# A two-layer graph kernel: layer 1's attention loop taken by pairs of units, in bfloat16 halves

## The chip, the cores and the metric

The kernel runs on one core of one Trainium2 chip. The metric is the time of one execution on the device, in microseconds; the kernel before takes 824.5 us (median of 3 runs, 824.09 to 824.69).

## The reference

x is 2708 x 128 and adj a 0/1 matrix of 2708 x 2708. Both layers end in a layer norm.

```python
# layer 0: x = layernorm(x + diffusion + sigmoid(alpha) * (softmax(beta * sim * adj) @ x - x))
# layer 1, with A = adj and X the result of layer 0:
XW = X @ W
s_col = XW @ a[0, :f]; s_row = XW @ a[0, f:]
Z1  = leaky_relu(s_row[:, None] + s_col[None, :], negative_slope=0.01)
den = exp(Z1)
num = A @ den
att = where(num != 0, den / where(num != 0, num, 1.0), 0.0)
H   = A @ (att @ XW)
x   = layernorm(X + H)
```

## The kernel before

Nodes are padded to 22 tiles of 128; the free axis of 2708 columns is cut into six chunks of 452 or 448 columns (`CH`). AT holds the transposed adjacency in SBUF as bfloat16. The order of the work is written out by hand: each engine has its own program, and engines meet only at semaphores, so an engine that waits holds up everything behind it in its program. The PE (TensorE) writes PSUM, which has eight banks.

**Layer 0** (until about 241 us) computes the softmax attention. Its last part ("the tail of layer 0", 241 to 372 us) runs over 22 row tiles: PE multiplies AT by x (`spread`, L1298), DVE (VectorE) adds the parts and takes mean and variance (`norm_in`: L797, L799, and L801 which adds epsilon), POOL (GpSimd) takes the power -0.5 (L391), and one tile later DVE subtracts the mean and multiplies (`x1_rows`, L809). Between these DVE runs the ranking steps (L832 to L854) by which both keys of layer 1 are sorted.

**Between the layers** (372 to 460 us) rows of AT are gathered in the sorted order by POOL's indirect DMAs (L411), and PE computes block sums (L1411). Since both keys are sorted, exp of the leaky relu splits into sums over blocks above and below a threshold, taken from a table `tab` (one product, L1471), except in the few tiles that the threshold crosses. For these the dense values `den` are computed, and multiplied with AT in a loop over tiles whose bounds are read into registers (L1478).

**Layer 1's loop** (460.6 to 728.8 us) has 132 units (`UNITS`): 22 column tiles `jt` times six chunks. PE goes by pairs `v` of units, 66 in all: `num(v)` puts two numerators into banks 6 and 7: two table products (L1471), four products for each crossed tile (two bfloat16 parts of `den` for each of two chunks, L1478), and two tiny closing matmuls (L1482). For each unit ACT (ScalarE) takes the logarithm (L589), DVE forms the score z (L1122) and subtracts the logarithm (L1136), ACT takes the exponential with a bias (L595), and PE multiplies by XW in float32 (L1492) into banks 0 to 5, two pairs behind `num` (`LAG`). There are seven slots for z and three for logarithms, of 452 columns each. DVE forms two scores ahead:

```python
for u in (2 * v, 2 * v + 1):
    if u + 2 < NU:
        attention_scores(u + 2)
    dv.wait_ge(s_ln, u + 1)
    V.tensor_tensor(z_of(u), z_of(u), l_of(u), ALU.subtract)
```

Once for each `jt`, `den_scores` (L1052, L1056) prepares the next tile's `den` on DVE behind two register loads and a branch, ACT takes its exponential (L568), and `den_halves` splits it (L1067, L1069). `den_all` (not entered here) is a branch in the third pair of each `jt`.

XW in sorted order comes by 22 indirect DMAs that POOL issues from 461.5 us on (L417), after the last block sum; the product of tile `jt` waits for its own DMA only.

**The end**: banks 0 to 5 are copied to YT (DVE L1147, ACT L603), transposed by PE (L1505), copied again (L1156, L608), written to DRAM in two DMAs (SP, L302 and L305), gathered by 22 indirect DMAs of POOL (L427), split by DVE (L759, L761) in four slices (`SL`), and multiplied with AT (L1516 for the first six row tiles, slice by slice; `spread`, L1298, for the other 16). The layer norm follows, with the power on POOL (L433) and the last step on DVE (L1173).

## Time and profile before

| | us |
|---|---|
| median of 3 runs | 824.5 |
| profiled execution | 824.38 |
| its span on the core | 822.6 |
| PE busy | 702.5 (85%) |
| DVE busy | 649.6 (79%) |
| ACT busy | 448.6 (55%) |
| POOL busy | 284.4 (35%) |

The profiled execution takes 1.8 us more than its span; it lies within the three runs. Busy shares are averages over stages that have different limits, so the stages are to be looked at one by one. Matmuls are pipelined: the duration of one is longer than the distance to the next, and the distance is what a stream of them costs. Of the 22 column tiles of layer 1's loop, 19 have two crossed tiles, one (jt 8) has three, and two (jt 20 and 21) have one, as the count of L1478 between two table products shows (8, 12 and 4).

### The profile page before, as it was taken

The page shows a single profiled execution, that of the slowest core. Times are in us where ns is not written, and L with a number is a line of the kernel's source. Part 1 is how long each engine was busy: PE and PEld are TensorE (multiplying, and loading weights), DVE is VectorE, ACT ScalarE, POOL GpSimd, SP SyncE. Part 2 cuts the span into 40 slices and gives each one's busy share as a digit, 9 for nine tenths or more (in the row PEclk, how much of TensorE's full clock was granted, in tenths as well). Part 3 has the DMA queues.
Part 4 walks back from the last instruction along what each step waited for, and adds up shares of the span by engine and source line. Part 5 has one row for each costly group of instructions (what it writes and reads, how often), then busy time and mean ns, then how long its engine had stood idle before and what let it go on. Part 6 is the DMA issues. An engine that isn't in the chain of part 4 may idle for free.

```text
span 822.6 us, 13449 instructions
## 1 busy us (share of the span) xinstructions
PE 702.5 (85%) x4380; PEld 385.1 (47%) x4380; DVE 649.6 (79%) x1428; ACT 448.6 (55%) x705; POOL 284.4 (35%) x294
## 2 busy tenths in 40 slices
PE   5599999999969888843799899999999999965895
PEld 5243334333338777732345344444444444433684
DVE  3599999999987799998966778776777777862584
ACT  2398888888851156785202466665666666740000
POOL 5378888787760211112820460000000000007431
PEclk9999999999977999955799999999999999986998
DMA  9953454980000000021970010000000000023110
GB/s 209 207 98 68 78 92 77 408 328 1 1 4 1 14 22 14 14 84 52 372 321 0 24 49 0 1 1 0 1 2 1 0 2 1 0 71 120 32 39 20
DMA packets 24552, 58.22 MB, mean 71 GB/s; under 512 B 2634, under 2 KB 13918, under 8 KB 24478
## 3 DMA queue, kind: packets, MB, share of 16 engines
q0 software_dynamic: 7744, 33.39, 16.0%
q1 hardware_dynamic: 16734, 23.92, 8.1%
q8 instruction: 37, 0.61, 0.3%
q14 instruction: 37, 0.30, 0.1%
HBM read 51.59 MB, written 20.96 MB: 88 GB/s over the span
## 4 chain that ended last, share of the span: by engine, by line
PE 54%; DVE 28%; issue 10%; POOL 3%; ACT 2%; DMA 2%; DVEq 0%; POOLq 0%; SPq 0%; ACTq 0%
PE PSALL L1492 14%; PE PSALL L1478 13%; PE PSALL L1298 8%; DVE ring L724 7%; DVE R L733 6%; PE PSALL L1411 5%; PE PSALL L1471 3%; PE PSALL L1278 2%; DVE R L845 2%; PE PSALL L1226 2%; POOL X L427 2%; DVE XN L845 1%; PE PSALL L1354 1%; PE PSALL L1516 1%; PE PSALL L1482 1%
## 5 line engine op out<-in xcount | busy, mean ns | idle before, releaser
L369 POOL TENSOR_TENSOR R<-R,ring 128x452 f32<-128x452 f32 (+1 forms) x126 | 151.6, 1204 | 33.2 <-ACT ring L462 31.5
L733 DVE SCALAR_TENSOR_TENSOR R<-ring,R 128x452 bf16<-128x452 f32 (+1 forms) x132 | 134.6, 1021 | 0.0
L1478 PE MATMUL PSALL<-AT,R 128*128 x516 | 117.4, 355 | 4.1 <-issue 1.4
L1278 PE MATMUL PSALL<-R,AO 128*128 128x452 bf16 (+2 forms) x396 | 98.9, 359 | 16.8 <-DVE R L733 15.7
L462 ACT ACTIVATE ring<-ring,sm 128x452 f32<-128x452 f32 (+1 forms) x132 | 88.4, 670 | 27.8 <-DVE ring L724 21.0
L1226 PE MATMUL PSALL<-XN 128*128 128x452 f16 (+2 forms) x396 | 98.4, 358 | 4.7 <-issue 4.2
L1298 PE MATMUL PSALL<-R,AT 128*128 128x256 f16 (+1 forms) x836 | 102.1, 284 | 0.0
L470 ACT ACTIVATE R<-ring,sm 128x452 bf16<-128x452 f32 (+1 forms) x132 | 88.6, 671 | 4.3
L1298 PEld LDWEIGHTS PSALL<-R,AT 128*128 128x128 bf16 (+1 forms) x836 | 83.8, 102 | 12.8 <-issue 0.2
L1492 PE MATMUL PSALL<-ring,X 128*128 128x452 f32 (+1 forms) x188 | 84.8, 567 | 0.0
L423 POOL MEMSET R<- 128x108 f32 x1 | 0.2, 188 | 237.9 <-PE PSALL L1492 237.9
L724 DVE TENSOR_TENSOR ring<-PSALL,AT 128x452 f32<-128x452 f32 (+1 forms) x132 | 81.0, 614 | 0.9 <-PE PSALL L1226 0.9
L1478 PEld LDWEIGHTS PSALL<-AT,R 128*128 x516 | 49.4, 96 | 65.0 <-issue 40.8
L595 ACT ACTIVATE ring<-ring,st 128x452 f32<-128x452 f32 x94 | 62.9, 671 | 25.4 <-DVE ring L1136 25.4
L1122 DVE SCALAR_TENSOR_TENSOR ring<-R,st 128x452 f32<-128x452 f32 x94 | 64.1, 682 | 0.0
L1278 PEld LDWEIGHTS PSALL<-R,AO 128*128 128x128 bf16 (+1 forms) x396 | 28.5, 97 | 73.9 <-DVE R L733 59.6
L1226 PEld LDWEIGHTS PSALL<-XN 128*128 128x128 f16 (+1 forms) x396 | 32.6, 97 | 51.0 <-DVE ring L724 28.4
L1411 PE MATMUL PSALL<-AT,X 128*128 128x452 bf16 (+1 forms) x264 | 53.0, 362 | 2.2 <-DVE X L984 2.2
L391 POOL TENSOR_TENSOR ln<-ln,sm 128x1 f32<-128x1 f32 (+1 forms) x22 | 13.7, 621 | 97.4 <-DVE ln L801 97.4
L529 ACT ACTIVATE XN<-R 128x128 bf16<-128x128 bf16 (+20 forms) x28 | 37.9, 1354 | 15.7 <-DVE R L845 14.1
L589 ACT ACTIVATE ring<-PSALL,sm 128x452 f32<-128x452 f32 x44 | 27.8, 633 | 26.9 <-PE PSALL L1482 26.9
L1492 PEld LDWEIGHTS PSALL<-ring,X 128*128 128x128 f32 x188 | 32.0, 189 | 19.5 <-issue 18.0
(247 smaller groups left out, 1100.1 us busy)
## 6 DMA issues: line engine op xcount, KB each, us to landing
AT<-in_adjT POOLq DMA_DIRECT2D x22, 677.0 KB, 7.4
ATd<-AT SPq DMA_DIRECT2D x2, 7447.0 KB, 31.0
XWd<-ring SPq DMA_DIRECT2D x11, 128.0 KB, 1.8
x1d<-AO SPq DMA_DIRECT2D x1, 1408.0 KB, 5.8
out<-ring SPq DMA_DIRECT2D x21, 64.0 KB, 1.5
Yd<-R SPq DMA_DIRECT2D x1, 768.0 KB, 3.7
Yd<-R SPq DMA_DIRECT2D x1, 640.0 KB, 3.6
AT<-ATd,idx POOLq DMA_INDIRECT x22, 10.4
```

Of the source, the lines that this page charges most:

```text
L369: i = G.tensor_tensor(ES_, ES_, z, ALU.add)
L462: S.activation(z, z, ACT.Exp, scale=bcol[0:rows, :]).then_inc(s_exp, 1)
L470: S.activation(fh, z, ACT.Identity, bias=mone[0:rows, :]).then_inc(s_exp, 1)
L724: V.tensor_tensor(z, PSALL[0:rows, b, 0:w], A_, ALU.mult).then_inc(s_z, 1)
L733: V.scalar_tensor_tensor(F[0:rows, RW:RW + w], z, 1.0, F[0:rows, 0:w], ALU.subtract, ALU.subtract).then_inc(s_low, 1)
L1122: V.scalar_tensor_tensor(z_of(u), rb[:, c0:c0 + w], c99[:, jt:jt + 1], rb01[:, c0:c0 + w], ALU.add, ALU.max).then_inc(s_z1, 1)
L1226: m = TE.matmul(PSALL[0:rows, b, 0:w], lh[:, jt * P:jt * P + rows], rh[:, c0:c0 + w], start=(k == 0), stop=(k == 2))
L1278: m = TE.matmul(PSALL[:, c, 0:w], half_[0:rows, jt, :], F[0:rows, o:o + w], start=(jt == 0 and k == 0), stop=(jt == T - 1 and k == 2))
L1298: ins = TE.matmul(PSALL[0:m, bank, 0:2 * D], AT[:, jt, it * P:it * P + m], parts[:, jt, :, :].rearrange("p c d -> p (c d)"), start=(jt == ...
L1411: m = TE.matmul(PSALL[:, c, 0:w], W3[q][:, t * P:(t + 1) * P], AT[:, t, c0:c0 + w], start=(t == 0 and q == 0), stop=(t == T - 1 and q == 1))
L1478: TE.matmul(PSALL[:, b, 0:w], d, AT[:, bass.ds(k, 1), c0:c0 + w].rearrange("p o j -> p (o j)"), start=False, stop=False)
L1492: TE.matmul(PSALL[:, c, 0:CH[c][1]], XWs[:, jt, :], z_of(u), start=(jt == 0), stop=(jt == T - 1)).then_inc(s_y, 1)
```

## The change

Layer 1's loop goes by pairs on all engines. A score, a logarithm, a subtraction and an exponential now cover two chunks, 904 (or 900) columns, in one instruction. There are four slots for z and one for the logarithm. The term of slope 0.01 of the row is taken out of the loop (`erb`, multiplied in when PSUM is read at the end) and that of the column too, so the score is a tensor_scalar (add, max with 0) and the exponential has no bias.

The exponential's float32 is read as two bfloat16 halves in place: the upper 16 bits are `high`, and DVE writes z minus high into the lower 16 bits (`attention_low`, new; one per pair). POOL splits XW in the same way (`XWh`, three instructions a tile), after it has issued all 22 indirect DMAs. The product of a unit becomes three bfloat16 matmuls in place of one in float32.

Where exactly two tiles are crossed, `num` runs eight products and the two table products in line, without loop and closing matmuls; otherwise the old loop runs. `den` is split in place too: three tensor_scalar, one exponential, one subtraction.

At the end DVE alone reads the six banks, pair by pair as they are done, PE transposes into six banks of their own, ACT alone copies them; eight row tiles, not six, are multiplied slice by slice. The last step of both layer norms moves from DVE to POOL, with the addition of epsilon, and DVE's tensor_reduce of the last tail becomes a scalar_tensor_tensor. Small operations between the layers are rearranged.

```diff
+        den_w = R1[:, DEN0:DEN0 + NDEN * P].rearrange("p (t j) -> p t j", t=NDEN)
+        den_h = R1[:, DEN0:DEN0 + NDEN * P].bitcast(BF16).rearrange("p (t j c) -> p t j c", t=NDEN, c=2)
...
-        slots = [ring[:, 5, :], R1[:, rest:rest + RW]] + [AO[:, q * RW:(q + 1) * RW] for q in range(3)]
-        slots += [ring[:, q, :] for q in range(5)]
-        NZ, NL = 7, 3
-        tL, tZ = slots[0:NL], slots[NL:]
+        pairs = [RF[:, 0:2 * RW], RF[:, 2 * RW:4 * RW], AO[:, 0:2 * RW], RF[:, 4 * RW:6 * RW]]
+        NZ = 4
+        tL = R1[:, rest:rest + 2 * RW]
+        XWh = X[:, :].bitcast(BF16).rearrange("p (t d c) -> p t d c", t=T, c=2)
...
+        def halves_of(v):
+
+            both = z_of(v).bitcast(BF16).rearrange("p (n c) -> p n c", c=2)
+            return both[:, :, 1], both[:, :, 0]
...
+                mean, var, rstd = moments(it)
+                gp.wait_ge(s_tail, TAIL * it + 4)
+                G.tensor_scalar(rstd, var, LN_EPS, None, ALU.add).then_inc(s_rstd, 1)
+                gp.wait_ge(s_rstd, 2 * it + 1)
+                G.tensor_tensor(rstd, rstd, mhalf[0:m, :], ALU.pow).then_inc(s_rstd, 1)
+                gp.wait_ge(s_ao, 12)
+                if it == T - 1:
+                    G.memset(AO3[:, it, :], 0.0).then_inc(s_x1, 1)
+                    gp.wait_ge(s_x1, T)
+                gp.wait_ge(s_rstd, 2 * it + 2)
+                G.tensor_scalar(AO3[0:m, it, :], hc[0:m, s, :], mean, rstd, ALU.subtract, ALU.mult).then_inc(s_x1, 1)
...
+            gp.wait_ge(s_ohl[1], T)
+            gp.wait_ge(s_perm[1], 2)
+            for t in range(T):
+                gp.wait_ge(s_AT[t], 48)
+                if t:
+                    gp.wait_ge(s_xws, 3 * t)
+                G.tensor_copy(iota[:, :], XWs[:, t, :]).then_inc(s_xws, 1)
+                gp.wait_ge(s_xws, 3 * t + 1)
+                G.tensor_tensor(XWh[:, t, :, 0], XWs[:, t, :], iota[:, :], ALU.subtract).then_inc(s_xws, 1)
+                gp.wait_ge(s_xws, 3 * t + 2)
+                G.tensor_copy(XWh[:, t, :, 1], iota[:, :]).then_inc(s_xws, 1)
...
+            gp.wait_ge(s_y, NV)
+            gp.wait_ge(s_sub, NV)
+            G.memset(YT[:, N:NP], 0.0).then_inc(s_pad, 1)
...
-                for u in (2 * v, 2 * v + 1):
-                    av.wait_ge(s_num, u + 1)
-                    if u < NL:
-                        av.wait_ge(s_E, 1)
-                        av.wait_ge(s_winset, 2)
-                    else:
-                        av.wait_ge(s_sub, u - NL + 1)
-                    av.wait_ge(s_const, CONST)
-                    S.activation(l_of(u), PSALL[:, 6 + u % 2, 0:CH[UNITS[u][1]][1]], ACT.Ln, bias=tiny).then_inc(s_ln, 1)
+                av.wait_ge(s_num, v + 1)
+                if v:
+                    av.wait_ge(s_sub, v)
+                else:
+                    av.wait_ge(s_E, 1)
+                av.wait_ge(s_const, CONST)
+                S.activation(tL.rearrange("p (q w) -> p q w", q=2), PSALL[:, 6:8, 0:RW], ACT.Ln, bias=tiny).then_inc(s_ln, 1)
                 if cp == 0 and jt + 1 < T:
                     den_exp(jt + 1, 0)
-                for u in (2 * v, 2 * v + 1):
-                    av.wait_ge(s_sub, u + 1)
-                    av.wait_ge(s_c99, 2)
-                    S.activation(z_of(u), z_of(u), ACT.Exp, bias=c01[:, jt:jt + 1]).then_inc(s_att1, 1)
+                av.wait_ge(s_sub, v + 1)
+                S.activation(z_of(v), z_of(v), ACT.Exp).then_inc(s_att1, 1)
...
+                    for q in range(WN):
+                        V.tensor_scalar(den_w[:, s + q, :], cb3[:, jt, :], rsrt[:, q:T][:, bass.ds(where["base"], 1)],
+                                        r01[:, q:T][:, bass.ds(where["base"], 1)], ALU.add, ALU.max).then_inc(s_denz, 1)
...
-                    V.tensor_copy(den_b[:, s:s + WN, 0, :], fw3).then_inc(s_denb, 1)
-                    dv.wait_ge(s_denb, DENB * jt + 1)
-                    V.tensor_tensor(den_b[:, s:s + WN, 1, :], fw3, den_b[:, s:s + WN, 0, :],
-                                    ALU.subtract).then_inc(s_denb, DENB - 1)
+                    V.tensor_tensor(den_h[:, s:s + WN, :, 0], den_w[:, s:s + WN, :], den_h[:, s:s + WN, :, 1],
...
-                V.scalar_tensor_tensor(z_of(u), rb[:, c0:c0 + w], c99[:, jt:jt + 1], rb01[:, c0:c0 + w],
-                                       ALU.add, ALU.max).then_inc(s_z1, 1)
-
-            for u in range(2):
-                attention_scores(u)
+                    dv.wait_ge(s_y, v - NZ + 1)
+                V.tensor_scalar(z_of(v), rb[:, c0:c0 + w], c99[:, v // 3:v // 3 + 1], 0.0, ALU.add, ALU.max).then_inc(s_z1, 1)
+
+            def attention_low(v):
+
+                high, lower = halves_of(v)
+                dv.wait_ge(s_att1, v + 1)
+                V.tensor_tensor(lower, z_of(v), high, ALU.subtract).then_inc(s_alo, 1)
+
+            attention_scores(0)
             for v in range(NV):
                 jt, cp = v // 3, v % 3
+                if v:
+                    attention_low(v - 1)
+                if v + 1 < NV:
+                    attention_scores(v + 1)
                 if cp == 0 and jt + 1 < T:
                     den_scores(jt + 1)
-                for u in (2 * v, 2 * v + 1):
-                    if u + 2 < NU:
-                        attention_scores(u + 2)
-                    dv.wait_ge(s_ln, u + 1)
-                    dv.wait_ge(s_z1, u + 1)
-                    V.tensor_tensor(z_of(u), z_of(u), l_of(u), ALU.subtract).then_inc(s_sub, 1)
+                dv.wait_ge(s_ln, v + 1)
+                dv.wait_ge(s_z1, v + 1)
+                V.tensor_tensor(z_of(v), z_of(v), tL[:, 0:wide_of(v)[1]], ALU.subtract).then_inc(s_sub, 1)
...
+                    V.tensor_tensor(YT[:, c0:c0 + w].rearrange("p (q w) -> p q w", q=2), PSALL[:, 2 * p:2 * p + 2, 0:RW],
+                                    erb[:, c0:c0 + w].rearrange("p (q w) -> p q w", q=2), ALU.mult).then_inc(s_YTd, 2)
...
+                V.scalar_tensor_tensor(h, ps[:, 0:D], down_y[0:m, :], AO3[0:m, it, :], ALU.mult, ALU.add).then_inc(s_tail1, 1)
+                dv.wait_ge(s_tail1, TAIL * it + 1)
+                V.scalar_tensor_tensor(h, ps[:, D:2 * D], down_y[0:m, :], h, ALU.mult, ALU.add).then_inc(s_tail1, 1)
...
+                with eng.If(reg["off"] >= TWO):
+                    first = nc.s_assert_within(reg["lo"], 0, T - WN, skip_runtime_bounds_check_because="two tiles from there")
+                    for q in range(2):
+                        for part in (1, 0):
                             for b, c0, w in pair:
-                                TE.matmul(PSALL[:, b, 0:w], d,
-                                          AT[:, bass.ds(k, 1), c0:c0 + w].rearrange("p o j -> p (o j)"),
-                                          start=False, stop=False)
-                for b, c0, w in pair:
-                    TE.matmul(PSALL[:, b, 0:1], U[0:1, :], ones[0:1, :], start=False, stop=True).then_inc(s_num, 1)
+                                TE.matmul(PSALL[:, b, 0:w], den_h[:, s + q, :, part],
+                                          AT[:, q:T, c0:c0 + w][:, bass.ds(first, 1), :].rearrange("p o j -> p (o j)"),
+                                          start=(q == 0 and part == 1), stop=False)
+                    for b, c0, w in pair:
+                        m = TE.matmul(PSALL[:, b, 0:w], EX[:, jt * P:(jt + 1) * P], tab[:, c0:c0 + w], start=False, stop=True)
+                    m.then_inc(s_num, 1)
+                pe.only(met)
+                with eng.Else():
...
-                    for u in (2 * (v - LAG), 2 * (v - LAG) + 1):
-                        jt, c = UNITS[u]
-                        pe.wait_ge(s_att1, u + 1)
-                        pe.wait_ge(s_AT[jt], 48)
-                        TE.matmul(PSALL[:, c, 0:CH[c][1]], XWs[:, jt, :], z_of(u),
-                                  start=(jt == 0), stop=(jt == T - 1)).then_inc(s_y, 1)
-
-
-            pe.wait_ge(s_YTa, 3)
-            pe.wait_ge(s_YTd, 3)
-            pe.wait_ge(s_ypad, 1)
+                    p = v - LAG
+                    jt, high, lower = p // 3, *halves_of(p)
+                    pe.wait_ge(s_alo, p + 1)
+                    pe.wait_ge(s_xws, 3 * (jt + 1))
+                    for q in range(2):
+                        c = 2 * (p % 3) + q
+                        part_of = slice(q * RW, q * RW + CH[c][1])
+                        for k, (part, att) in enumerate(((1, high), (1, lower), (0, high))):
+                            m = TE.matmul(PSALL[:, c, 0:CH[c][1]], XWh[:, jt, :, part], att[:, part_of],
+                                          start=(jt == 0 and k == 0), stop=(jt == T - 1 and k == 2))
+                    m.then_inc(s_y, 1)
...
-                for it in range(6):
+                for it in range(8):
```

## Rows read from the trace of the kernel before

**Rows 1.** Windows, layer 1's loop: PE, PEld, DVE, ACT, POOL, then clock and DMA
```profile
492.20:728.80 236.60, 233.52 (x932) 101.30 (x930) 177.22 (x308) 152.72 (x255) 0.01 (x1) 1.00 0.00 1
```

**Rows 2.** Chain of waits in one pair (start us, us, what)
```profile
576.13 1.71 PE PSALL L1492 x4
577.85 0.38 PE PSALL L1471 x2
```

**Rows 3.** PE timeline, table products at the start of four column tiles
```profile
485.92 0.54 PE L1471 MATMUL PSALL<-R,AO 128*128 128x452 bf16 x2
...
498.09 0.54 PE L1471 MATMUL PSALL<-R,AO 128*128 128x452 bf16 x2
...
706.54 0.55 PE L1471 MATMUL PSALL<-R,AO 128*128 128x452 bf16 x2
...
716.16 0.54 PE L1471 MATMUL PSALL<-R,AO 128*128 128x452 bf16 x2
```

**Rows 4.** DVE by line and form (busy us, mean ns | idle before)
```profile
L1136 DVE TENSOR_TENSOR ring<-ring 128x452 f32<-128x452 f32 x31 | 19.4, 626 | 6.1 <-ACT ring L589 5.8
L1069 DVE TENSOR_TENSOR R<-R 128x384 bf16<-128x384 f32 x22 | 12.4, 563 | 2.3
L845 DVE TENSOR_SCALAR R<-R,st 128x896 bf16<-128x896 f32 x2 | 1.4, 686 | 0.0
L1173 DVE TENSOR_SCALAR ring<-ring,ln 128x128 f32<-128x128 f32 x21 | 7.1, 337 | 0.0
```

**Rows 5.** ACT by line and form over the span
```profile
L589 ACT ACTIVATE R<-PSALL,sm 128x452 f32<-128x452 f32 x44 | 27.9, 633 | 15.0 <-PE PSALL L1482 15.0
L568 ACT ACTIVATE R<-R 128x384 f32<-128x384 f32 x22 | 11.5, 523 | 5.1 <-DVE R L1056 5.1
L556 ACT ACTIVATE R<-R 128x2816 f32<-128x2816 f32 x1 | 2.5, 2550 | 40.4 <-DVE R L1024 40.4
```

**Rows 6.** Timeline of DVE and ACT in two pairs
```profile
572.96 0.68 DVE L1122 SCALAR_TENSOR_TENSOR ring<-R,st 128x452 f32<-128x452 f32 x1
573.56 0.62 DVE L1136 TENSOR_TENSOR ring<-ring,AO 128x448 f32<-128x448 f32 x1
...
574.22 0.67 ACT L595 ACTIVATE ring<-ring,st 128x448 f32<-128x448 f32 x1 [0.46 <-DVE ring L1136]
...
574.61 0.56 DVE L1052 TENSOR_TENSOR R<-XN,st 128x384 f32<-128x384 f32 x1 [0.43 <-issue]
```

**Rows 7.** POOL timeline, first and last of the 22 gathers of XW
```profile
461.51 0.94 POOL L417 DMA_INDIRECT X<-XWd,idx  x1 [43.60 <-PE PSALL L1411]
...
489.76 1.08 POOL L417 DMA_INDIRECT X<-XWd,idx  x1 [0.30 <-issue]
```

**Rows 8.** POOL by line and form over the span
```profile
L391 POOL TENSOR_TENSOR ln<-ln,sm 128x1 f32<-128x1 f32 x21 | 12.1, 576 | 92.4 <-DVE ln L801 92.4
L352 POOL TENSOR_TENSOR AO<-X,AO 128x2304 bf16<-128x2304 f32 x1 | 5.0, 5039 | 8.4 <-ACT AO L449 8.4
L391 POOL TENSOR_TENSOR ln<-ln,sm 20x1 f32<-20x1 f32 x1 | 1.6, 1578 | 5.0 <-DVE ln L801 5.0
```

**Rows 9.** Timeline of DVE in one tile of layer 0's tail
```profile
304.03 0.18 DVE L799 BATCH_NORM_AGGREGATE ln<-ln 128x2 f32<-128x6 f32 x1
...
304.57 0.29 DVE L832 SCALAR_TENSOR_TENSOR ring<-R,ident 128x128 bf16<-128x128 f32 x1
```

**Rows 10.** Windows: layer 0's tail, and the end
```profile
340.00:350.00 10.00, 9.08 (x103) 7.53 (x102) 9.72 (x37) 7.48 (x12) 1.15 (x2) 0.86 0.05 15
739.80:771.00 31.20, 16.72 (x106) 12.52 (x107) 9.05 (x14) 0.00 (x0) 21.80 (x22) 0.69 0.31 93
```

**Rows 11.** Timeline at the end of the loop: last DMA of Y, first gather
```profile
735.94 0.36 SPq L305 DMA_DIRECT2D Yd<-R  x1
...
739.79 0.95 POOL L427 DMA_INDIRECT X<-Yd,idx  x1 [10.81 <-DMA Yd<-R]
```

**Rows 12.** PE timeline, the last two row tiles of the last stage
```profile
807.82 5.07 PE L1298 MATMUL PSALL<-R,AT 128*128 128x256 f16 x44
```

More of the change, by code:

```diff
@@ L252, in adj_resnorm2_kernel @@
         W_IN = 16 * len(SMALL)
-        TAIL = 5
+        TAIL = 4
         behind = {}
@@ new lines, in num @@
+                pe.only(met)
+                with eng.Else():
+                    for b, c0, w in pair:
+                        TE.matmul(PSALL[:, b, 0:w], EX[:, jt * P:(jt + 1) * P], tab[:, c0:c0 + w], start=True, stop=False)
+                    with eng.If(reg["lo"] < reg["hi"]):
+                        with eng.Fori(reg["lo"], reg["hi"]) as k:
+                            at = nc.s_assert_within(k + reg["off"], 0, NDEN - 1, skip_runtime_bounds_check_because="a window tile, or one of all")
+                            for part in (1, 0):
+                                d = den_h[:, bass.ds(at, 1), :, part].rearrange("p o j -> p (o j)")
+                                for b, c0, w in pair:
+                                    TE.matmul(PSALL[:, b, 0:w], d,
+                                              AT[:, bass.ds(k, 1), c0:c0 + w].rearrange("p o j -> p (o j)"),
+                                              start=False, stop=False)
+                    for b, c0, w in pair:
+                        m = TE.matmul(PSALL[:, b, 0:1], U[0:1, :], ones[0:1, :], start=False, stop=True)
+                    m.then_inc(s_num, 1)
@@ L1484, in _ @@
+                pe.only(met)
             for v in range(NV + LAG):
```

295 lines of the change are left out of this document (128 added, 167 removed).

## Prediction

> **What bounds the kernel now.** I read the windows first. In layer 1's loop PE is busy 233.5 of 236.6 us at full clock and DVE 177.2 [rows 1], so PE sets the pace there. The chain of waits says with what: of one pair's chain 1.71 us are the products in float32 (L1492), two units in four records, and 0.38 us two bfloat16 products, 0.19 us each [rows 2]. The PE timeline gives the pace: a column tile with two crossed tiles takes 498.09 - 485.92 = 12.17 us, one with a single crossed tile 716.16 - 706.54 = 9.62 us [rows 3]. In the tail of layer 0 DVE is the bound, 9.72 of 10 us [rows 10]. In the last stage it is PE again: 44 products in 5.07 us, 0.11 us each in a stream, 2.42 us a row tile [rows 12]. Before it PE waits for the gathers of Y: 16.7 of 31.2 us busy, clock 0.69 [rows 10].
>
> **PE's part of the change, alone.** Six bfloat16 products take the place of 1.71 us: 6 x 0.19 = 1.14 us. In line, `num` is ten products, 1.9 us. That is 3.1 us a pair where 12.17 / 3 = 4.06 us are spent now. If PE stayed the bound the loop would shrink by some 60 us. It doesn't, by the order in which DVE and ACT are now written.
>
> **The ring of DVE and ACT.** In the new loop DVE does, in this order, `attention_low(v-1)`, `attention_scores(v+1)`, the subtraction of v. `attention_low(v-1)` waits for the exponential of v-1, and that waits for the subtraction of v-1. So from one subtraction to the next there lie, one after the other, the subtraction, the exponential, the low half and a score, with nothing of the loop's DVE work to put under the exponential except `den_halves`. Before, DVE formed scores and went on while ACT worked. The price:
> - subtraction, 904 columns: L1136 is 626 ns at 452 and L1069 563 ns at 384, 0.93 ns a column; at most 1.04, which 904 columns in 0.63 + 452 x 1.04 would make. I take 1.10 us [rows 4].
> - exponential without bias: L568 is 523 ns at 384 columns, L556 2550 at 2816, 0.83 ns a column: 0.96 us [rows 5].
> - low half: the same form as L1069 (float32 and bfloat16 in, bfloat16 out), 1.10 us, less the 0.08 us by which the next DVE instruction starts early (572.96 + 0.68 against 573.56) [rows 6]: 1.02.
> - score: now a tensor_scalar of float32; L845 with 896 columns takes 686 ns, so 0.69, less 0.08: 0.61 us [rows 4].
> - two hops between engines: L1136 ends at 574.18, L595 starts at 574.22, 0.04 us each [rows 6].
>
> Sum: 1.10 + 0.04 + 0.96 + 0.04 + 1.02 + 0.61 = 3.77 us a pair. Once a column tile `den_scores` stands in the ring too: the register loads and branch cost 0.43 us of idle and the 0.08 of overlap (574.18 to 574.61 [rows 6]), and three tensor_scalar of 128 columns 0.26 each (337 ns less 0.08 [rows 4]): 1.28 us. `den_halves` (0.56) fits under the exponential. A column tile takes 3 x 3.77 + 1.28 = 12.59 us, against 12.17 for two crossed tiles and 9.62 for one.
>
> Does anything else hold the ring? The logarithm of 904 columns costs 0.63 + 452 x 0.83 = 1.01 us [rows 5], starts behind the exponential, and ends 0.6 us before DVE wants it. PE's `num(v+1)` starts behind the logarithm of v, say 0.5 us later for the branch (bounds 0 and 1), and takes 1.9: it is done by the time ACT comes to it. So PE will stand idle a fifth of the time. With three crossed tiles (jt 8) one more costs (12.17 - 9.62) / 3 = 0.85 us a pair in the old branch, and PE with the logarithm becomes the bound; I add 2.4 us for it.
>
> **The start of the loop.** The first product waits for `XWh` of tile 0, and POOL splits it only behind all 22 gathers in its own program. The first gather is issued at 461.51, the last at 489.76, done at 490.8 [rows 7]; in the kernel before the product waits for its own tile's gather only. With DVE idle the gathers may go at 0.94 + 0.30 each, ending at 488.5; I take 489.7. Three POOL instructions of 128 columns at 2.19 ns (L352, 5039 / 2304 [rows 8]) and 0.1 us each, 1.1 us: 490.8. PE has `num(0)` to `num(2)` behind it by about 469 and idles; after such a gap its clock is low (0.69 over the gathers of Y, a mean of 1.2 and 2.4 GHz [rows 10]). At half clock the first product takes 2.3 us and `num(3)` 3.8, the logarithm 1.0: subtraction 3 starts at 498. Behind PE's wait stand `num(3)` and with it every later logarithm, and DVE can't run ahead: score 4 needs the slot that product 0 frees. By the ring alone subtraction 3 would start near 476.5, my estimate from the sums above.
>
> From 498: 62 intervals x 3.77 = 233.7, 19 `den_scores` x 1.28 = 24.3, and 2.4: the last subtraction starts at 758.4, its low half ends 3.24 later at 761.6, the last product at 762.8. That is **34.0 us later** than 728.8.
>
> **The end of the loop.** DVE now reads the banks pair by pair behind the last low half: 1.10 + 1.02 + two of 0.54 is 3.2 us, the last transposes 0.9, ACT's last copies 1.0: the second DMA of Y is issued 5.2 us behind the last low half, 766.8; before at 735.94 [rows 11], 7.1 us behind the last product. So 3.1 us come back here; 30.9 us are left. From there to the first gather it is 3.85 us as before [rows 11], and the 22 gathers are untouched.
>
> **The last stage.** Two row tiles (2 x 2.42 = 4.84 us) move into the wait for the gathers, which has 14 us of idle PE [rows 10]; behind the last slice 8 more products stand (0.9). Gain 3.9 us. The last tile's layer norm on POOL costs 0.3 us more.
>
> **Layer 0's tail.** L801 and L809 leave DVE. L799 ends at 304.21 and L832 starts at 304.57; L832 would start at 304.13: 0.44 us a tile [rows 9]. DVE is the bound where the ranking steps stand beside the tiles (the code has them from tile 5 on, 17 tiles): 7.5 us; I take 7.0 (bounds 0 and 10), since ACT comes near (7.5 of 10 us busy [rows 10]). POOL's part is 0.15 + 0.58 + about 0.4 us a tile where a tile takes 4 to 5.
>
> POOL and DVE do disturb each other: L391 takes 576 ns as a rule and 1578 ns once [rows 8]. The Trainium skill (SBUF — State Buffer, "SBUF: two separate sides") says that GpSimd and VectorE's two-port instructions lock one pair of ports for a whole instruction and the other fully blocks. By that rule the moved work could block DVE up to 0.4 us a tile and the tail would gain nothing. The row agrees that POOL waits; that DVE does, no row shows.
>
> **Between the layers** the new exponential `erb` costs 2.5 us by L556, where ACT waited 40.4 us [rows 5]; uncovered it would cost these 2.5. The small DVE operations there replace others, under PE's block sums. POOL's 66 instructions for `XWh` (24 us) lie beside the loop, where POOL had nothing to do [rows 1]; only the first three are waited for. Nothing for all of these.
>
> **Sum**, against the profiled execution's own 824.4 (span 822.6 and 1.8 around it; the median of the runs is 824.5): 824.4 - 7.0 + 30.9 - 3.9 + 0.3 = 844.7. **I predict 844.5 us**, 2.4% slower. Its own range is 835 to 854: 0.1 us a pair in the ring is 6.5 us, the start 3, `den_scores` 0.4 us x 19.
>
> **Rivals.**
> - *Tail of layer 0 gains nothing* (port pair): 824.4 + 30.9 - 3.6 = 851.7. For it L391's long case, against it that L832 keeps its 0.29 us while POOL works. Chance 0.10.
> - *Branches cost more* in the ring (register loads for three addresses in `den_scores`, PE's jump behind the logarithm's wait, beyond the 1.4 us that PE and ACT have in hand): 0.25 us a pair is 16 us, 860. Chance 0.10.
> - *The score runs at one column a cycle*, as L1122 does (0.68 us at 452 columns [rows 6]): 1.15 for 0.69 us, 62 x 0.46 = 29 us more, 873. Against it L845. Chance 0.04.
> - *PE's clock falls* in the loop because PE idles. At half clock 16 products take 6.1 us and PE is the bound again: 62 x 1.9 us more, 963. Against it: at 9.08 of 10 us busy the clock was 0.86, not half [rows 10]. Chance 0.04.
> - *The other side: the ring doesn't close*, and PE sets the pace at 3.3 us a pair. Then the loop behind the start takes 62 x 3.3 = 205 in place of 260 us: 790. It needs DVE to have other work under the exponential; it decides the sign once the ring falls by 20.3 / 62 = 0.33 us a pair, to 3.44. Against it the order in which the code is written. Chance 0.05, and 0.03 for a time within 0.2% of before.
>
> A time within 0.2% is what this kernel's measurement can't tell from no change. The forecast has 0.64; with the first two rivals 0.84. The range 829 to 863 takes these in. Faster 0.05, same 0.03, slower 0.92.
>
> **What the profile after should show.** Between subtractions of one column tile 3.77 us, 12.6 us a column tile whatever the number of crossed tiles; before nearly each exponential ACT waits for DVE and before each low half DVE waits for ACT by about 1 us; PE busy under 85% in the loop; PE idle from about 462 to 484 us (469 to 491, less the 7 of layer 0), with POOL's gathers as the reason; tiles of layer 0's tail 0.44 us shorter. It is wrong if DVE shows no idle before the low half, if the score takes over 1 us, or if the first product starts before the last gather.

## The result and the profile after

The changed kernel takes 848.34 us (median of 4 runs, 846.65 to 849.68) against 824.6 for the kernel before (median of 4 runs beside it): ratio 1.0286 (95% interval 1.0268 to 1.0303), 2.9% slower, where 2.4% were forecast. The profiled execution took 848.36 us, its span is 846.5 us, 23.9 more than before. First the same window of the loop as in [rows 1]:

```profile
492.20:728.80 236.60, 193.80 (x937) 89.01 (x935) 184.78 (x246) 115.58 (x133) 37.09 (x57) 1.00 0.01 1
```

PE is busy 193.8 of 236.6 us where it was busy 233.5, DVE 184.8 where it was 177.2, at a full granted clock (1.00). No engine is full. The timeline of DVE and ACT shows one turn of the ring of waits that the prediction describes (start us, us, engine and line; in brackets the idle time before and who ended it):

```profile
559.34 1.09 DVE L1152 TENSOR_TENSOR AO<-AO,R 128x904 f32<-128x904 f32 x1
560.47 0.96 ACT L633 ACTIVATE AO<-AO 128x904 f32<-128x904 f32 x1 [0.48 <-DVE AO L1152]
561.45 1.19 DVE L1139 TENSOR_TENSOR AO<-AO 128x904 bf16<-128x904 f32 x1 [1.02 <-ACT AO L633]
562.55 0.67 DVE L1133 TENSOR_SCALAR ring<-R,st 128x900 f32<-128x900 f32 x1
563.14 1.08 DVE L1152 TENSOR_TENSOR ring<-ring,R 128x904 f32<-128x904 f32 x1
...
566.95 1.08 DVE L1152 TENSOR_TENSOR ring<-ring,R 128x900 f32<-128x900 f32 x1
...
571.52 1.08 DVE L1152 TENSOR_TENSOR ring<-ring,R 128x904 f32<-128x904 f32 x1
```

Read each line by its bracket: the exponential (L633) waits for the subtraction (L1152), the low half (L1139) waits 1.02 us for the exponential, and the score (L1133) and the next subtraction follow without a gap. Subtractions come 3.80 and 3.81 us apart, 4.57 where `den_scores` stands between them: 12.18 us a column tile.

The start of the loop, in the timelines of POOL, PE and DVE:

```profile
486.85 0.94 POOL L437 DMA_INDIRECT X<-XWd,idx  x1 [0.31 <-issue]
487.80 0.30 POOL L448 CAST iota<-X 128x128 bf16<-128x128 f32 x1
488.18 0.43 POOL L450 TENSOR_TENSOR X<-X,iota 128x128 bf16<-128x128 f32 x1
488.68 0.32 POOL L452 COPY X<-iota 128x128 bf16<-128x128 bf16 x1
489.15 2.42 PE L1524 MATMUL PSALL<-ring,X 128*128 128x452 bf16 x6 [22.72 <-POOL X L452]
491.52 3.06 PE L1488 MATMUL PSALL<-AT,R 128*128 x8
496.05 1.10 DVE L1152 TENSOR_TENSOR ring<-ring,R 128x904 f32<-128x904 f32 x1 [1.68 <-ACT R L629]
```

POOL issues its last gather at 486.85 us, splits tile 0, and only then PE starts, after 22.72 us of idle time, at the lower of its two clocks (granted 0.50, that is 1.2 GHz, from 489 to 492 us; 2.42 us for six products that later take 1.36). The subtraction at 496.05 us is that of pair 3; the one of pair 2 started at 467.52.

The end, in the timelines of PE, SP and POOL, beside [rows 11, 12]:

```profile
753.96 2.43 PE L1524 MATMUL PSALL<-ring,X 128*128 128x452 bf16 x6 [1.78 <-DVE ring L1139]
760.14 0.36 SPq L316 DMA_DIRECT2D Yd<-R  x1
764.74 1.00 POOL L460 DMA_INDIRECT X<-Yd,idx  x1 [8.09 <-DMA Yd<-R]
791.28 10.55 PE L1543 MATMUL PSALL<-R,AT 128*128 128x256 f16 x80 [2.45 <-DVE R L792]
801.67 33.88 PE L1310 MATMUL PSALL<-R,AT 128*128 128x256 f16 x308
838.17 0.80 POOL L472 TENSOR_SCALAR ring<-ring,ln 20x128 f32<-20x128 f32 x1
```

### The profile page after: what moved, and what is told of

Read it like the earlier page. It is cut to its first block, busy times and chain, and to the rows that moved or that the text cites. A ratio compares the mean times of both kernels' runs of the same rounds, so it can differ in the third digit from the quotient of the medians.

```text
span 846.5 us, 12916 instructions
## 1 busy us (share of the span) xinstructions
PE 662.7 (78%) x4404; PEld 371.6 (44%) x4404; DVE 638.2 (75%) x1276; ACT 413.6 (49%) x574; POOL 392.6 (46%) x449
## 4 chain that ended last, share of the span: by engine, by line
DVE 39%; PE 21%; issue 16%; POOL 10%; ACT 9%; DVEq 2%; DMA 2%; POOLq 0%; ACTq 0%; SPq 0%
DVE ring L755 6%; DVE R L764 6%; DVE ring L1152 6%; PE PSALL L1423 5%; ACT ring L633 5%; POOL X L437 3%; PE PSALL L1310 3%; DVE ring L1133 3%; PE PSALL L1238 2%; PE PSALL L1290 2%; DVE R L867 2%; POOL X L460 2%; POOL ring L472 2%; DVE AO L1152 2%; ACT AO L633 2%
## 5 line engine op out<-in xcount | busy, mean ns | idle before, releaser
L1488 PE MATMUL PSALL<-AT,R 128*128 x432 | 93.4, 359 | 41.1 <-ACT R L629 39.6
L1290 PE MATMUL PSALL<-R,AO 128*128 128x452 bf16 (+2 forms) x396 | 99.9, 362 | 15.7 <-DVE R L764 14.6
L1310 PE MATMUL PSALL<-R,AT 128*128 128x256 f16 (+1 forms) x792 | 94.0, 279 | 0.0
L1139 DVE TENSOR_TENSOR ring<-ring 128x904 bf16<-128x904 f32 (+1 forms) x50 | 60.5, 1209 | 42.8 <-ACT ring L633 42.8
L1524 PE MATMUL PSALL<-ring,X 128*128 128x452 bf16 (+1 forms) x300 | 70.1, 369 | 25.4 <-POOL X L452 22.7
L633 ACT ACTIVATE ring<-ring 128x904 f32<-128x904 f32 (+1 forms) x50 | 47.8, 956 | 72.9 <-DVE ring L1152 72.9
L629 ACT ACTIVATE R<-PSALL,sm 128x904 f32<-128x904 f32 x66 | 66.0, 1000 | 35.6 <-PE PSALL L1492 26.7
L1488 PEld LDWEIGHTS PSALL<-AT,R 128*128 128x128 bf16 x432 | 41.2, 98 | 94.0 <-issue 67.2
L1152 DVE TENSOR_TENSOR ring<-ring,R 128x904 f32<-128x904 f32 (+1 forms) x50 | 55.5, 1110 | 2.7 <-ACT R L629 2.7
L1524 PEld LDWEIGHTS PSALL<-ring,X 128*128 128x128 bf16 x300 | 28.8, 98 | 55.9 <-issue 24.6
L1133 DVE TENSOR_SCALAR ring<-R,st 128x904 f32<-128x904 f32 (+1 forms) x50 | 34.8, 697 | 20.8 <-PE PSALL L1524 20.8
```

The lines of the kernel that those rows point to most:

```text
L633: S.activation(z_of(v), z_of(v), ACT.Exp).then_inc(s_att1, 1)
L1152: V.tensor_tensor(z_of(v), z_of(v), tL[:, 0:wide_of(v)[1]], ALU.subtract).then_inc(s_sub, 1)
L1290: m = TE.matmul(PSALL[:, c, 0:w], half_[0:rows, jt, :], F[0:rows, o:o + w], start=(jt == 0 and k == 0), stop=(jt == T - 1 and k == 2))
L1310: ins = TE.matmul(PSALL[0:m, bank, 0:2 * D], AT[:, jt, it * P:it * P + m], parts[:, jt, :, :].rearrange("p c d -> p (c d)"), start=(jt == ...
L1488: TE.matmul(PSALL[:, b, 0:w], den_h[:, s + q, :, part], AT[:, q:T, c0:c0 + w][:, bass.ds(first, 1), :].rearrange("p o j -> p (o j)"), star ...
L1524: m = TE.matmul(PSALL[:, c, 0:CH[c][1]], XWh[:, jt, :, part], att[:, part_of], start=(jt == 0 and k == 0), stop=(jt == T - 1 and k == 2))
```

## Experiments

Twelve more kernels were timed, in three sets of four, counting the changed kernel and the kernel before once more. In the first and the third set the kernel before took 851.0 us (849.8 to 852.8) and 851.1 us (842.6 to 853.5), in the second 824.7 us (823.8 to 825.9), so totals are compared within a set only, and with care even there (more on this below). For a comparison across the sets I read one stretch in each trace, **the loop**: from the first gather of XW to the last product (POOL's memset behind it marks that end). Beside it stands the pace, the time of a column tile with two crossed tiles.

| kernel | set | median us | ratio to before (95%) | loop us | pace us |
|---|---|---|---|---|---|
| before | 2 | 824.7 | | 267.8 | 12.2 |
| changed, again | 2 | 847.22 | 1.0276 (1.0257 to 1.0294) | 299.3 | 12.18 |
| XW split early | 1 | 843.01 | 0.990 (0.987 to 0.993) | 275.4 | 12.20 |
| the same again | 3 | 841.76 | 0.9896 (0.987 to 0.9922) | 276.6 | 12.20 |
| low half later | 1 | 840.98 | 0.9887 (0.9867 to 0.9908) | 276.1 | 11.20 |
| both | 1 | 821.58 | 0.9649 (0.9629 to 0.967) | 255.2 | 11.20 |
| both again | 3 | 820.55 | 0.9648 (0.9584 to 0.9713) | 255.1 | 11.20 |
| two products more | 1 | 865.62 | 1.0172 (1.0153 to 1.0192) | 300.7 | 12.22 |
| float32, no halves | 2 | 785.09 | 0.9513 (0.9497 to 0.9529) | 237.9 | 10.36 |
| float32, low half kept | 3 | 839.88 | 0.9871 (0.9804 to 0.9939) | 273.7 | 12.18 |
| float32, norm on DVE | 3 | 812.93 | 0.957 (0.9498 to 0.9641) | 248.6 | 10.36 |
| both norms on DVE | 2 | 847.32 | 1.0272 (1.0247 to 1.0297) | 300.2 | 12.2 |

The changed kernel's first trace has 300.6 and 12.18, the first one of before 267.3 (461.51 to 728.79).

**XW split early.** POOL splits tile t three gathers behind its own instead of behind all 22.

```diff
-            for t in range(T):
-                G.indirect_dma_start(out=XWs[:, t, :], ...)
             gp.wait_ge(s_ohl[1], T)
             gp.wait_ge(s_perm[1], 2)
-            for t in range(T):
+            for n in range(T + 3):
+                if n < T:
+                    G.indirect_dma_start(out=XWs[:, n, :], ...)
+                t = n - 3
+                if t < 0:
+                    continue
                 gp.wait_ge(s_AT[t], 48)
```

> The changed kernel, but POOL splits XW of tile t three gathers behind its own gather instead of behind all 22. My theory: the wait of PE for XWh of tile 0 costs the loop what the trace of the changed kernel shows, subtraction 3 at 496.05 us where the ring alone would have it at 467.52 + 3.80 + 0.76 = 472.1 us, so 24 us are saved: 824 us (822 to 828), product 0 at about 466 us, pairs still 3.8 us from subtraction to subtraction. Rival (the start is bound by something else too, such as the products' own data or POOL and DVE blocking each other): less than 12 us are saved, 836 us or more.

> The early split alone, once more, beside the kernel before at 824.7. From first gather to last product 275.3 us on the first chip, 25.3 less than the changed kernel: 847.8 - 25.3 = 822.5 us, 821 to 825. Rival: it keeps the 0.990 of the first run, 816.

PE's first product has no wait left in front of it, and subtraction 3 (of pair 3) stands 4.8 us behind subtraction 2 instead of 28.5 (496.05 - 467.52):

```profile
477.95 1.37 PE L1525 MATMUL PSALL<-ring,X 128*128 128x452 bf16 x6
479.10 1.11 DVE L1153 TENSOR_TENSOR AO<-AO,R 128x900 f32<-128x900 f32 x1
483.89 1.09 DVE L1153 TENSOR_TENSOR ring<-ring,R 128x904 f32<-128x904 f32 x1
```

The loop is 25.2 and, the second time, 24.0 us shorter, the pace unchanged. The wait at the start costs 24 to 25 us, as expected. Both totals are 19 us above what was expected (824, and 822.5 the second time), and the second kept the ratio 0.990, as its rival had it; that belongs to sets 1 and 3, of which more below.

**The low half later.** On DVE the low half of v-1 is done behind the subtraction of v, so that something lies beside the exponential.

```diff
-                if v:
-                    attention_low(v - 1)
                 if v + 1 < NV:
                     attention_scores(v + 1)
 ...
                 V.tensor_tensor(z_of(v), z_of(v), tL[:, 0:wide_of(v)[1]], ALU.subtract).then_inc(s_sub, 1)
+                if v:
+                    attention_low(v - 1)
```

> The changed kernel with one instruction of DVE's program moved: the low half of pair v-1 stands behind the subtraction of v, not ahead of it; the work is the same. Theory of the ring (subtraction, exponential, low half, score one after the other): the exponential now lies beside a score and the next subtraction, DVE has 3.3 us of work a pair, ACT and PE each a chain of about 3.2 to 3.4 us, so the mean pair falls from 4.06 to about 3.4 us, 62 x 0.66 = 41 us: 807 us (802 to 815). Rival (DVE's own busy time, or PE's branches, or lower clock sets the 4.06 us): the order changes nothing, 845 to 850 us.

The ring opens: the loop is 24.5 us shorter with the same wait at the start. But 41 were expected. The timelines of PE and ACT show what holds it now:

```profile
561.94 1.37 PE L1524 MATMUL PSALL<-ring,X 128*128 128x452 bf16 x6
563.30 1.70 PE L1488 MATMUL PSALL<-AT,R 128*128 x8
564.84 0.55 PE L1492 MATMUL PSALL<-R,AO 128*128 128x452 bf16 x2
565.35 1.38 PE L1524 MATMUL PSALL<-AO,X 128*128 128x452 bf16 x6
567.61 1.70 PE L1488 MATMUL PSALL<-AT,R 128*128 x8 [0.89 <-issue]
...
562.01 1.02 ACT L629 ACTIVATE R<-PSALL,sm 128x904 f32<-128x904 f32 x1 [0.28 <-PE PSALL L1492]
565.42 1.02 ACT L629 ACTIVATE R<-PSALL,sm 128x904 f32<-128x904 f32 x1 [0.27 <-PE PSALL L1492]
```

From product to product it is 565.35 - 561.94 = 3.41 us, and once a column tile 0.89 us of PE's own issue, where its three register loads stand. 3 x 3.41 + 0.9 = 11.1. I had expected 3.4 us for every pair and nothing for the loads.

The 3.41 us are not PE's work, though. Six products take (1.37 - 0.36) / 5 = 0.20 us each from start to start (one record lasts 0.36), the ten of the numerator 0.19 each: 3.1 us. What sets 3.41 is a second ring, between PE and ACT. A numerator may go into banks 6 and 7 only when the logarithm has read the last one (`pe.wait_ge(s_ln, v)`), and the logarithm waits for the whole numerator. The numerator takes 564.84 + 0.55 - 563.30 = 2.09 us, the logarithm starts 0.03 later and takes 1.02, and the next numerator starts 0.27 behind its end (562.01 + 1.02 against 563.30), where PE's branch stands: 3.41 us. PE's product fits into the gap.

**Both.**

> Both edits: XW split three gathers behind, and the low half behind the next subtraction. If wait and ring are separate causes the gains add: 848 - 24 - 41 = 783 us (778 to 792), faster than both kernels. If they are one cause (the start only loses what the ring would lose anyway) it is not better than the better of the two alone, about 807 us.

> The early split together with the low half behind the subtraction, once more, beside the kernel before at 824.7: its first run stood on a chip on which the kernel before took 851. From first gather to last product it took 255.1 us there against 300.6 in the changed kernel, 45.5 less: 847.8 - 45.5 = 802 us, 800 to 805, if nothing of the loop came from that chip. Rival: it keeps the 0.965 of the first run, 796.

The loop is 45.4 us shorter in both runs, 4 us short of the sum of the two alone (25.2 + 24.5), and no run says why; the median is 3.5% below before's in the same sets. The expected 783 was too low by some 20 us for the register loads on PE and 19 for the set; the repetition missed its 802 in the same way and kept its ratio.

**Two products more on PE** in each pair of the branch for two crossed tiles, started before the numerator and overwritten by it:

```diff
                 with eng.If(reg["off"] >= TWO):
+                    for b, c0, w in pair:
+                        TE.matmul(PSALL[:, b, 0:w], EX[:, jt * P:(jt + 1) * P], tab[:, c0:c0 + w], start=True, stop=True)
```

> The changed kernel with two more bfloat16 products of 452 columns a pair on PE, in the branch with two crossed tiles, 0.38 us more for 57 of the 66 pairs, into banks that the next products overwrite. Theory of the ring: PE has 0.55 us in hand between the end of a numerator and the logarithm that reads it, so nothing changes beyond the stall's end at low clock (0 to 2 us): 848 to 851 us. Rival (PE with its waits and branches paces the loop): 57 x 0.38 = 22 us more, 870 us.

```profile
557.69 1.13 DVE L1152 TENSOR_TENSOR ring<-ring,R 128x904 f32<-128x904 f32 x1
...
569.93 1.11 DVE L1152 TENSOR_TENSOR AO<-AO,R 128x904 f32<-128x904 f32 x1
```

12.24 us a column tile, and a loop of 300.7 us: 0.38 us of PE work more in such a pair costs 0.1 us in all. PE doesn't set the pace of the changed kernel. The median is near the rival's 870, but not for its reason: it is 15 us above the 848 to 851 expected because of the set: that kernel's first gather of XW comes at 465.86 us, 10 later than the changed kernel's, and the other 5.6 us are lost behind the loop.

**The changed kernel and before again**, the second set's references:

> The changed kernel once more, nothing edited, as the reference beside the other three. Two theories of the first four experiments, whose traces show TensorE waiting in single products (up to 1.75 us each, released by nothing the profile shows) at 403 to 413 us and again in the last stage, about 10 and 6 us together, which the changed kernel's first trace doesn't show. (a) It is a property of the chip or the moment, code of TensorE loaded while the indirect gathers fill the DMA queues: then this kernel shows the same stalls on the same chip, about 862 to 866 us, and the kernel before also stands near 851; on a chip without them 848 and 824.6, ratio 1.029. (b) It came with the edits: then this kernel is at 848 here as well, whatever the kernel before does.

> The kernel before once more, for its trace on this chip. If the stalls belong to the chip, they stand in this trace too: TensorE waiting inside the products of 403 to 413 us and beside the gathers of Y, and the rest of the trace as in the first one (loop from first gather to last product 267 to 268 us). If it is at 824.6, none of them stands there.

Neither kernel shows the stalls here, and the times are those of the first runs. Theory (b) falls, since the kernel before, which has none of the edits, also took 851 us in set 1. That the same stalls made it so isn't shown: in sets 1 and 3 it has no trace. All eight traces of these sets have them; here PE of the float32 kernel with the low half:

```profile
405.76 0.35 PE L1411 MATMUL PSALL<-AT,X 128*128 128x452 bf16 x1 [1.06 <-issue]
407.17 0.35 PE L1411 MATMUL PSALL<-AT,X 128*128 128x452 bf16 x1 [1.06 <-issue]
409.27 0.54 PE L1411 MATMUL PSALL<-AT,X 128*128 128x452 bf16 x1 [1.75 <-issue]
```

PE gets single products with up to 1.75 us between them while POOL's gathers of AT run, and again beside the gathers of Y. In these eight traces the first gather of XW comes 9 to 12 us later than in the changed kernel's own two, and the stretch behind the loop is 6 to 9 us longer: 16 to 20 us together, which is the excess over the expected times of the two early-split runs and most of it elsewhere. The kernel before lost 26 us in the same sets, so their ratios flatter the changed kernels: "two products more" stands at 1.017 with a loop as long as that of the changed kernel, which stands at 1.028. The loops and paces are what the argument rests on.

**Float32, no halves.** Everything of the new loop is kept, but PE multiplies attention and XW in float32, so that neither low half nor split is needed; POOL's split is taken out too (not shown).

```diff
-                if v:
-                    attention_low(v - 1)
 ...
-                    pe.wait_ge(s_alo, p + 1)
-                    pe.wait_ge(s_xws, 3 * (jt + 1))
+                    pe.wait_ge(s_att1, p + 1)
+                    pe.wait_ge(s_AT[jt], 48)
 ...
-                        for k, (part, att) in enumerate(((1, high), (1, lower), (0, high))):
-                            m = TE.matmul(PSALL[:, c, 0:CH[c][1]], XWh[:, jt, :, part], att[:, part_of],
-                                          start=(jt == 0 and k == 0), stop=(jt == T - 1 and k == 2))
+                        m = TE.matmul(PSALL[:, c, 0:CH[c][1]], XWs[:, jt, :], z_of(p)[:, part_of],
+                                      start=(jt == 0), stop=(jt == T - 1))
```

> The changed kernel with float32 products of attention and XW in place of the bfloat16 halves: no low half on VectorE, no split of XW on GpSimd, everything else of the new loop kept (it computes the same output). My theory: the ring of VectorE and ScalarE falls to 3.80 - 1.10 = 2.7 us a pair and stops to bind, TensorE does, with 1.9 (num) + 0.1 (den) + 1.71 = 3.7 to 3.9 us a pair, 11.9 us a column tile with two crossed tiles; and the wait of 20 us at the start goes since the product needs its own gather only. From the first gather of XW to the last product 262 to 272 us in place of 300.6, so 29 to 38 us less than the changed kernel. Rival: the in-line num with its branch costs more than its products; then over 280 us.

785.09 us, 4.9% faster than before and 62 us faster than the changed kernel, twice what I had expected. PE's timeline, and the window 500 to 600 us (PE, PEld, DVE, ACT, POOL, clock, DMA):

```profile
558.89 1.68 PE L1508 MATMUL PSALL<-ring,X 128*128 128x452 f32 x4
560.40 1.69 PE L1473 MATMUL PSALL<-AT,R 128*128 x8
561.93 0.55 PE L1477 MATMUL PSALL<-R,AO 128*128 128x452 bf16 x2
562.32 1.67 PE L1508 MATMUL PSALL<-AO,X 128*128 128x452 f32 x4
```

```profile
500.00:600.00 100.00, 99.20 (x404) 48.27 (x403) 58.94 (x92) 57.75 (x64) 0.00 (x0) 1.00 0.01 1
```

PE is full at 562.32 - 558.89 = 3.43 us a pair. From the start of the four float32 records to the next instruction it is 560.40 - 558.89 = 1.51 us, not the 1.68 of the record. Six bfloat16 products at 0.20 us are 1.20 (that the next numerator started 1.36 behind them above was its wait for the logarithm). So the halves save PE 0.3 us a pair of its own work, and even that not in time: with the ring of DVE opened, bfloat16 goes at 3.41 us a pair by the numerator and the logarithm, float32 at 3.43. My 3.7 to 3.9 us had added up record durations that overlap.

What makes this loop 30 us shorter than before's? PE is full in both (98.7 and 99.2 us of the window from 500 to 600), so PE's own stream got shorter. The kernel before, one pair:

```profile
577.68 0.55 PE L1471 MATMUL PSALL<-R,AO 128*128 128x452 bf16 x2
578.07 1.89 PE L1478 MATMUL PSALL<-AT,R 128*128 x8
579.89 0.20 PE L1482 MATMUL PSALL<-ones,U 1*128 1x1 bf16 x2
580.02 1.78 PE L1492 MATMUL PSALL<-ring,X 128*128 128x452 f32 x4
581.64 0.55 PE L1471 MATMUL PSALL<-R,AO 128*128 128x452 bf16 x2
```

The same eight products of `den` take 1.82 us in the loop over tiles and 1.53 in line, the closing matmuls 0.13 and nothing, the float32 product 1.62 and 1.51. These 0.53 us a pair, and more where a column tile starts, are the step from 12.17 to 10.36 us. The column tile with three crossed tiles (jt 8) is the counter-test within the same trace: there the float32 kernel goes through the old branch, and takes 15.7 us (541.25 to 556.96) where the kernel before took 15.0 (558.44 to 573.46). So it is the numerator written in line that shortens the loop; the batching of DVE and ACT by pairs brings nothing by itself, as they were not the bound.

**Float32 with the low half kept** on DVE in its place in the ring, nothing else of the halves:

```diff
-                    pe.wait_ge(s_xws, 3 * (jt + 1))
+                    pe.wait_ge(s_AT[jt], 48)
```

(and the float32 product and the removed split of the kernel above.)

> The changed kernel with float32 products and without the split of XW, but with VectorE's low half kept where the change has it, and the product waiting for it. The low half overwrites the tile that the float32 product then reads, so the output is off by what the low bits carry. It differs from the float32 experiment (785.1 us, 240 us from first gather of XW to last product) by the low half alone. My theory: the ring of subtraction, exponential, low half and score is what binds, so the 3.8 us a pair come back and the loop takes 275 us as with the early split, total 820 to 824. Rival: the loss came from what TensorE has to do for the halves (six products, branch) and VectorE's low half alone costs little; then 240 to 250 us and 785 to 795.

```profile
559.05 1.19 DVE L1127 TENSOR_TENSOR ring<-ring 128x904 bf16<-128x904 f32 x1 [1.02 <-ACT ring L621]
560.15 0.66 DVE L1121 TENSOR_SCALAR ring<-R,st 128x900 f32<-128x900 f32 x1
560.74 1.08 DVE L1140 TENSOR_TENSOR AO<-AO,R 128x904 f32<-128x904 f32 x1
```

The 1.02 us wait in front of the low half is back, the pace is 12.18 us again and the loop 273.7. One DVE instruction of 1.2 us a pair costs 35.8 us, with PE's products in either format. That separates the two costs: 300.6 - 273.7 = 26.9 us for the split, most of it the wait at the start, and 273.7 - 237.9 = 35.8 us for the ring. The two loops stand in different sets, but the paces agree across sets (10.36 us in sets 2 and 3 without the low half), and (12.18 - 10.36) x 20 tiles is 36 us. The total is 16 us and more above the 820 to 824 expected, as are the others of that set.

**Both layer norms' last step on DVE**, POOL keeping the addition and the power:

```diff
-                G.tensor_scalar(AO3[0:m, it, :], hc[0:m, s, :], mean, rstd, ALU.subtract, ALU.mult).then_inc(s_x1, 1)
 ...
-                G.tensor_scalar(h, h, mean, rstd, ALU.subtract, ALU.mult).then_inc(s_fin, 1)
 ...
                 norm_in(h, it, s_tail, TAIL * it + 2)
+                if it:
+                    x1_rows(it - 1)
 ...
                 norm_in(h, it, s_tail1, TAIL * it + 2)
+                if it:
+                    out_rows(it - 1)
```

> The changed kernel with the last step of both layer norms ((h - mean) times rstd) back on VectorE, GpSimd keeping the sum with epsilon and the power. Prediction's step: the step on GpSimd was worth 0.44 us a tile less on VectorE; that includes the fused addition. Undone, VectorE has 0.34 us a tile more: the first gather of XW comes 3 to 6 us later. In the last stage GpSimd's 0.80 us goes and the end behind the last product shrinks from 3.4 to 2.7 us, 0.7 less. Total plus 2 to plus 5 us. Rival (port pair): VectorE was blocked by GpSimd's step for about as long as it saved, first gather within 1 us of the changed kernel's, total minus 1 to plus 1.

The first gather of XW is issued at 457.57 us, in the changed kernel's two traces at 455.84 and 454.96: the step on POOL was worth 1.7 to 2.6 us, a little under the 3 to 6 expected. The last instruction ends 2.6 us behind the last product and not 3.4. From these two 1 to 2 us more would follow; the total, 847.3 against 847.2, shows nothing of them, with runs 3.5 us apart. POOL and DVE in one tile of the changed kernel:

```profile
342.90 2.58 POOL L405 TENSOR_TENSOR ln<-ln,sm 128x1 f32<-128x1 f32 x1
...
340.58 0.34 DVE L876 SCALAR_TENSOR_TENSOR ring<-R,st,ring 128x128 bf16<-128x128 f32 x1
...
340.85 0.45 DVE L876 SCALAR_TENSOR_TENSOR ring<-R,st,ring 128x128 bf16<-128x128 f32 x1
```

POOL's power takes 2.58 us beside two of DVE's tensor_scalar (L867, 1.21 us each), and 0.58 in the first tiles. DVE's second L876 falls beside POOL's step (0.97 us from 340.54) and takes 0.45 instead of 0.34; with the step on DVE both take 0.34.

**Float32 with the last layer norm's step on DVE**, to add that to the best kernel:

> The float32 experiment with the last step of the last layer norm back on VectorE. From the experiment with both steps on VectorE, where the end stood 2.6 us behind the last product in place of 3.4: 0.8 us less than 785.1, 784.3, the layer-0 part unchanged. Rival: VectorE, 0.3 us a tile busier, falls behind TensorE's 2.42 us a tile; it has over 1 us a tile in hand, so no.

The last instruction ends 2.6 us behind the last product, 3.5 in the float32 kernel, so the step is right: 0.9 us. The total, 812.93 for the 784.3 expected, shows nothing of it. It belongs to set 3, whose kernel before took 851, and this kernel's loop is 10.7 us longer than the float32 kernel's with the same code: ACT has two waits of 5.0 and 5.3 us between 479 and 493 us that the profile puts down to nothing on the core. So even a loop can be disturbed in these sets; no other trace of them has such waits in its loop.

## Why the prediction was right, point by point

| step | predicted | measured |
|---|---|---|
| tail of layer 0 | -7.0 | -5.7 (461.51 to 455.84) |
| loop to the last product | +34.0 | +33.3 |
| last product to the first gather of Y | -3.1 | -2.7 |
| first gather of Y to PE's last product | -3.9 | -2.3 |
| behind it | +0.3 | +1.2 |
| sum | +20.3 | +23.9 |

**The ring** is right in kind and in its sum: 3.80 us for 3.77. The low half takes 1.19 to 1.21 us where 1.10 was taken from L1069, the score 0.67, the exponential 0.96. `den_scores` costs 0.76 us and not 1.28: its register loads and branch don't show, only the three instructions (0.84, less the overlap). I read this as DVE's sequencer doing them while the low half and the score run; where DVE came straight out of a long wait, 0.86 us of issue do stand in front of them (at 493.16 us). 12.18 us a column tile for 12.59; over 20 tiles that is 8 us too much in the forecast. At jt 8 three crossed tiles take 14.25 us, 2.1 above the rest, for 2.4.

**The start** is right in kind, PE idle until POOL has issued all gathers, and 3.7 us too short: subtraction 3 at 496.05, in before's time 501.7, for 498. The error is in the gathers: the last one is done at 487.8, in before's time 493.5, where 489.7 was taken; those that ran beside the first three low halves took up to 1.89 us each. Behind it the first column tiles take 12.8 to 13.2 us, and in the float32 kernel with the low half, which has no split on POOL, 12.2: the split's 66 instructions beside DVE cost some 2 us, for which the forecast had nothing. So +33.3 for +34.0 is partly luck: the start and the split cost some 6 us more than forecast, `den_scores` 8 less.

**PE's part.** The halves were to bring PE's product from 1.71 to 1.14 us a pair; from start to start of neighbours it is 1.52 to 1.20. The numerator in line was priced rightly (1.92 us for 1.9). PE isn't the bound, so the error didn't show in the time.

**The end of the loop**: the last six products take 2.43 us at the lower clock (granted 0.50) where 1.2 was assumed; in the second trace of the same kernel they take 1.37 at 1.00, behind the same wait of 1.8 us. The transposes and copies come out as worked out (second DMA 3.7 us behind the last product, 7.1 before), though the terms given add up to 5.1 us and not 5.2. The first gather comes 4.6 us behind that DMA, for 3.85.

**The last stage** is the step that failed by a size: "behind the last slice 8 more products stand". The last slice has ten products for each row tile, so 20 more stand there, 80 against 60 in the trace of before:

```profile
766.00 8.36 PE L1516 MATMUL PSALL<-R,AT 128*128 128x256 f16 x60 [3.77 <-DVE R L761]
```

That is 10.55 us for 8.36, 2.2 and not 0.9. And POOL's last step takes 0.80 us where I had about 0.4, which with its addition makes the 0.9 us more behind the last product.

**Tail of layer 0**: from the twelve tiles between 303.38 and 355.91 us, 0.37 us a tile and not 0.44. With the last step back on DVE the same twelve take 1.9 us longer, 0.16 a tile, so more than half of the gain is not that step's but the rest of what left DVE there. POOL pays for sharing with 2.0 us in its power, and has the time; DVE pays 0.11 us of the 0.44. So the rival (no gain) was wrong. The Trainium skill (SBUF — State Buffer, "SBUF: two separate sides") says that GpSimd and a VectorE instruction in a two-port mode, or with two inputs in SBUF while GpSimd reads SBUF too, lock one pair of ports, and that whichever comes second fully blocks. For POOL the trace agrees: its power, 0.58 us otherwise, ends with DVE's second L867. For DVE it doesn't: L876 has two inputs in SBUF and starts at 340.85, while POOL's step, which reads SBUF, lasts until 341.51, so by the rule it would be held for 0.66 us, and the trace has 0.11.

**The rivals.** Branches cost less, not more. The score took 0.67 us for 904 columns, not 1.15. PE's granted clock stayed 1.00 in the loop at 0.82 busy. The other side is answered by the experiments: the ring does close, and once it is opened and the wait at the start is gone too, the loop falls to 255 us, below before's 267. The pace is then 3.41 us a pair for that rival's 3.3, set by the numerator and the logarithm and not by PE alone.

## What to carry to other kernels

Before a cheaper format is bought with extra work on another engine, write down the cycle of waits that the extra work joins: here 1.2 us of DVE stand between the exponential and the next subtraction and cost 36 us, while PE, for which it was meant, had 0.3 us less to do in a pair. When a ring is opened, look for the next one before the gain is forecast: here numerator and logarithm share two banks, and take 3.41 us a pair by themselves. Price a matmul from start to start of neighbours in a stream, not by its record, and ask of each operand prepared by another engine what else stands ahead of it in that engine's queue: 22 gathers in front of one split cost 25 us. Without the halves the rest of the change makes the kernel faster, 785 us; in the loop that is the numerator written in line.

## What the runs showed of the hardware

Register loads and a branch on DVE cost 0.43 us of idle time in the kernel before [rows 6] and 0.30 in the float32 kernel, none behind a low half and a score, and 0.86 behind a single score that had itself waited. On PE they don't show in the float32 kernel, whose products wait for nothing, and show as 0.89 us a column tile where the products wait for their low half; that PE's sequencer then has no lead is my reading.

A bfloat16 product of 452 columns takes 0.19 to 0.20 us from start to start, by a record of 0.36; the same product in float32 is two records, 0.38 us from start to start each.

POOL's indirect DMA takes 0.94 us with DVE idle. Beside DVE's work it mostly stays there in the kernel before and the float32 kernel (at most 1.6 us), and takes 1.3 to 2.1 us in the kernel with float32 products and the low half kept.

And the same kernel before took 3.2% longer in two sets of runs. In the traces of those sets PE gets its products one by one while indirect gathers run. The gathers alone don't do it: from 395 to 416 us the DMA queues move 416 GB/s in the changed kernel's first trace, which has no stalls, and 415 in the one shown above. That code is loaded late there is my reading, which no run here shows.
